# Cross attention and routed FFN on one core: an order of steps of its own for each engine in the attention stage, with routing arithmetic on GpSimd and the value product transposed by VectorE

## Chip, cores and metric

The kernel runs on one core of a Trainium2 chip. The metric is the device time of one execution in microseconds (us). A name such as L292 is line 292 of the kernel before; lines of the changed kernel are marked so. In the profile's rows PE is TensorE, PEld its weight loads, DVE is VectorE, ACT is ScalarE, POOL is GpSimd and SP is SyncE, which here only issues DMAs (SPq in the rows).

## What is computed

128 sequences of 128 tokens with 256 features pass through cross attention (16 heads of 16) and then a mixture of experts: 2 shared experts and, for each token, the best 4 of 16 routed ones. Cut to what matters:

```python
x = x + xattn(layernorm(x), ctx, ctx, Wq, Wk, Wv, Wo)     # softmax(q k^T / 4) v, heads joined, times Wo
h = layernorm(x)
shared = einsum(gelu(h @ shared_up), shared_down)          # 2 experts for every token
probs = softmax(h @ router_w.T); topk_p, topk_i = top_k(probs, 4)
routed = sum over the 4 of gate * (gelu(h @ routed_up[e].T) @ routed_down[e].T)
out = x + shared + routed
```

## The kernel before

The work has two stages on the same core.

**Attention stage.** The 128 sequences (batches n) go in 32 groups g of four (`GT = 4`). One list, `attention_steps()` (L46), is written out by hand, and every engine walks that same list and picks the steps that it has a part in (`run`, L278). Each engine executes its instructions strictly in its own program order and meets the others at semaphores: `fill[b]` and `drain[b]` say that PSUM bank b was written by TensorE and read out by its consumer, and `wait_free` (L275) holds TensorE at a bank until the step before on that bank is drained. The steps: `LN1`/`NA1` normalize x (statistics by VectorE, L750, square root by GpSimd, scaling by ScalarE), `XT` transposes it, `K0 K1 Q0 Q1 VA VB` project, `S` computes scores for the row maxima, `MT` transposes the maxima, `ST` computes the transposed scores less the maxima into banks 4 to 7, ScalarE exponentiates them (L645), `PV` multiplies by the values into bank 5. Then `OTR` (L499, four transposes on TensorE through bank 7 after a ScalarE copy), a division on VectorE (L786), `OT` (L506, two more transposes and a ScalarE copy) and `OP`, the output projection into bank 0, which VectorE adds to x (L798). `LN2`/`NA2` normalize the result into x2 (four buffers), `XT2`, `RL`, `R1`, `RK`, `R2` route: logits, the best four, a running count per expert, and each token's place in the table xs. R2 (L842) is a chain of some 20 small VectorE operations. `SC` (L995) are 512 indirect DMAs from GpSimd that scatter x2's rows into xs; each is also held back until TensorE has come to a certain step (L1005 to L1008).

SyncE issues the plain DMAs, all in one queue. In `LN2(g)` (L311) it waits for y (x plus attention) of group g and stores it, waits for the four `NA2` operations of the group and stores x2, and then issues `make_empty` (L324), a write of 2 MB of zeros for a later part of xs. `LN1(g)` (L299) loads x of group g into one of four buffers; since LN1(g+2) stands in the list where group g is worked on, its load comes behind the stores and the zeros of group g-1 in SyncE's program.

**FFN stage.** Blocks of 512 rows are read from xs, transposed, and multiplied by the expert's weights; 6 shared groups go ahead of the first routed block, then GpSimd gathers four rows for each token and VectorE sums them. VectorE drains the shared groups' down projections here (L928).

The lines that do the waiting of which this document speaks:

```python
def LN1(g):                                   # SyncE, L299
    wait(sp, y_kept[g % 4], 16 * (g // 4)); load_x(g)
def LN2(g):                                   # SyncE, L311
    sp.wait_ge(y_ready, GT * (g + 1));   sp.dma_start(yd ...)
    sp.wait_ge(xn2_ready, GT * (g + 1)); sp.dma_start(x2d ...); make_empty(g + 5)
def LN1(g):                                   # VectorE, L750
    dve.wait_ge(x_in[g % 2], 16 * (g // 2 + 1)); 4 x bn_stats; 4 x bn_aggr
```

Of the kernel before, what the change touches and what calls it, by code (L numbers as in the profile page):

```python
# [8 lines left out]
ALU = mybir.AluOpType  # L9
# [3 lines left out]
P = 128  # L13
# [27 lines left out]
ATT_BANKS = {"S": [0, 1, 2, 3], "K0": [4], "K1": [6], "Q0": [4], "Q1": [6], "VA": [4], "VB": [6], "PV": [5], "OTR": [7],  # L41
             "MT": [5], "OT": [7], "XT": [1, 2], "XT2": [1, 2], "RL": [1], "RK": [1], "OP": [0], "ST": [4, 5, 6, 7]}
# [3 lines left out]
def attention_steps():  # L46

    out = [("LN1", 0), ("NA1", 0), ("XT", 0), ("K0", 0), ("K1", 0), ("Q0", 0), ("Q1", 0), ("VA", 0), ("VB", 0), ("VA", 1), ("VB", 1),
           ("LN1", 1), ("NA1", 1), ("XT", 1), ("S", 0), ("MT", 0), ("ST", 0)]
    for n in range(B):  # L50
        g, i = divmod(n, GT)
        first, second, third, after = {
            0: (("K0", g + 1), ("K1", g + 1), ("RK", g - 2), [("R2", g - 2)]),
            1: (("Q0", g + 1), ("Q1", g + 1), ("XT2", g - 1), [("LN1", g + 2)]),
            2: (("VA", 2 * g + 2), ("VB", 2 * g + 2), ("RL", g - 1), []),
            3: (("VA", 2 * g + 3), ("VB", 2 * g + 3), ("XT", g + 2), [("LN2", g), ("R1", g - 1), ("WS", g)])}[i]
        s = TOPK * (n - 2 * GT - 1)
        out += [("S", n + 1), ("SC", s), first, ("PV", n), ("SC", s + 1)]
        if i == 2:
            out.append(("NA1", g + 2))  # L60
        out += [second, ("OTR", n)]
        if i == 0:
            out.append(("NA2", g - 1))
        out += [("SC", s + 2), third, ("OT", n), ("SC", s + 3), ("MT", n + 1), ("OP", n), ("ST", n + 1)]
        out += after
    g = G
    out += [("RK", g - 2), ("R2", g - 2), ("NA2", g - 1), ("XT2", g - 1), ("RL", g - 1), ("R1", g - 1), ("RK", g - 1), ("R2", g - 1)]
    out += [("SC", k) for k in range(TOPK * (B - 2 * GT - 1), TOPK * B)]
    last = {"SC": TOPK * B, "S": B, "MT": B, "ST": B, "VA": 2 * G, "VB": 2 * G}
    return [(name, n) for name, n in out if 0 <= n < last.get(name, B if name in ("PV", "OTR", "OT", "OP") else G)]  # L70
# [49 lines left out]
ATT = attention_steps()  # L120
# [946 lines left out]
```

## Time and profile before

| what | value |
|---|---|
| median of 3 runs | 2343.75 us (2338.73 to 2350.87) |
| the profiled execution | 2339.02 us, span 2336.8 us |
| busy share of the span: PE, DVE, ACT, POOL | 88%, 67%, 56%, 48% |
| chain that ended last | PE 58%, DVE 12%, POOL 9%, ACT 8%, DMA 7% |
| DMA | 486.46 MB, mean 208 GB/s |

The span is the time from the first instruction to the last in the profile. "Busy" is the union of an engine's instruction times; matmuls are pipelined, so that a row of merged matmuls overlaps the next one, and the spacing of the rows' starts tells what a step takes. The chain is followed back from the last instruction to what released each. A stretch of the page's 40 slices shows DMA share 0.2 to 0.5 up to slice 24, and about 0.9 behind it: the first is the attention stage, the second the FFN stage.

### The profile page before, as it was taken

To read this page: it belongs to the slowest core of one execution; us is meant where nothing else is said; L and a number is where in the kernel's file an instruction comes from. 1 tells how busy PE (TensorE), PEld (TensorE's weight loads), DVE (VectorE), ACT (ScalarE), POOL (GpSimd) and SP (SyncE) were. 2 spreads that over 40 slices of the span, in tenths; PEclk is the share of its full clock that TensorE was granted. 3 is DMA by queue.
4 is the path that set the end of the run, shared out by engine and by line. 5 is a ranking of instruction groups with operands and counts; after the bars stand their busy time and mean duration, and the time that the engine had idled before them with its cause. 6 is when DMAs were issued, how large, how long until landed. Compare 5 with 4: busy or idle time off the path is not lost.

```text
span 2336.8 us, 54349 instructions
## 1 busy us (share of the span) xinstructions
PE 2051.3 (88%) x20646; PEld 1549.3 (66%) x20646; DVE 1574.7 (67%) x4516; ACT 1304.9 (56%) x2364; POOL 1114.2 (48%) x1300
## 2 busy tenths in 40 slices
PE   5888898898888898998998886998999999989982
PEld 3565665665666666666666664687878778877872
DVE  3566666666666666666666656267878788877885
ACT  2445445455444545455545543398777767767772
POOL 1024344444344444444444444306666666666676
PEclk8999999999999999999999997999999999999996
DMA  7234534534534534534444434579999999989995
GB/s 270 78 111 149 167 127 149 176 128 144 178 128 139 174 123 143 174 123 149 164 139 159 143 114 154 202 278 326 332 340 330 338 323 343 332 296 344 328 331 176
DMA packets 242065, 486.46 MB, mean 208 GB/s; under 512 B 25873, under 2 KB 125202, under 8 KB 241810
## 3 DMA queue, kind: packets, MB, share of 16 engines
q1 hardware_dynamic: 192658, 348.71, 43.4%
q0 software_dynamic: 49152, 134.28, 17.3%
q8 instruction: 169, 2.77, 0.5%
q14 instruction: 86, 0.70, 0.1%
HBM read 214.98 MB, written 267.91 MB: 207 GB/s over the span
## 4 chain that ended last, share of the span: by engine, by line
PE 58%; DVE 12%; POOL 9%; ACT 8%; DMA 7%; issue 6%; DVEq 0%; POOLq 0%; SPq 0%; ACTq 0%
POOL gb L1023 9%; PE A L478 7%; PE A L400 7%; PE A L517 7%; PE A L604 6%; PE A L427 6%; DMA gb<-yl,idx 5%; PE A L581 5%; PE A L458 4%; PE A L495 4%; PE A L562 3%; DVE ms L776 3%; PE A L536 2%; ACT ot L657 2%; DVE rr L945 2%
## 5 line engine op out<-in xcount | busy, mean ns | idle before, releaser
L1009 POOL DMA_INDIRECT xs<-xn,idx x512 | 500.9, 978 | 608.2 <-DVE idx L881 187.2
L1023 POOL DMA_INDIRECT gb<-yl,idx x512 | 496.2, 969 | 343.9 <-issue 174.5
L648 ACT ACTIVATE pr<-A 128x512 f32<-128x512 f32 x512 | 264.3, 603 | 386.6 <-PE A L482 386.6
L776 DVE TENSOR_REDUCE ms<-A 128x4 f32<-128x512 f32 x512 | 316.7, 680 | 68.6 <-PE A L458 67.5
L945 DVE SCALAR_TENSOR_TENSOR rr<-gb,gate,rr 128x256 f32<-128x256 f32 x512 | 248.6, 486 | 140.0 <-DMA gb<-yl,idx 121.3
L604 PE MATMUL A<-wt,hh 128*128 128x256 f32 x1144 | 240.7, 294 | 3.7 <-DVE hl L925 3.7
L478 PE MATMUL A<-qt,km 32*128 32x128 f32 x4096 | 220.3, 334 | 0.6 <-DVE mt L796 0.6
L517 PE MATMUL A<-wos,ot 128*128 128x256 f32 x512 | 153.5, 425 | 76.4 <-ACT ot L657 76.4
L478 PEld LDWEIGHTS A<-qt,km 32*128 32x128 f32 x4096 | 183.8, 210 | 49.4 <-issue 45.5
L562 PEld LDWEIGHTS A<-ident,xr 128*128 128x128 f32 x1400 | 161.1, 142 | 82.7 <-issue 68.1
L562 PE MATMUL A<-ident,xr 128*128 128x128 f32 x1400 | 185.1, 276 | 34.0 <-DVE xl L914 29.9
L581 PE MATMUL A<-xh,wt 128*128 128x512 f32 x572 | 207.4, 403 | 0.0
L604 PEld LDWEIGHTS A<-wt,hh 128*128 128x128 f32 x1144 | 187.9, 191 | 4.4 <-DVE hl L925 4.3
L914 DVE TENSOR_TENSOR xl<-A,xh 128x512 fp32r<-128x512 f32 x286 | 182.8, 680 | 11.5 <-ACT xh L699 11.5
L801 DVE TENSOR_TENSOR xb<-A,xb 128x256 f32<-128x256 f32 x128 | 54.3, 424 | 193.0 <-PE A L517 193.0
L719 ACT ACTIVATE yo<-A 128x512 f32<-128x512 f32 x286 | 170.6, 598 | 20.6 <-PE A L604 6.0
L699 ACT ACTIVATE xh<-A 128x512 fp32r<-128x512 f32 x286 | 154.4, 594 | 24.4 <-PE A L562 24.2
L517 PEld LDWEIGHTS A<-wos,ot 128*128 128x128 f32 x512 | 90.8, 197 | 114.9 <-ACT ot L657 107.3
L604 PE MATMUL A<-wt,hl 128*128 128x256 f32 x572 | 161.9, 283 | 0.0
L691 ACT ACTIVATE wt<-wall 128x1024 fp32r x143 | 151.6, 1060 | 18.3 <-issue 14.4
L458 PE MATMUL A<-km,qt 32*128 32x256 f32 x2048 | 151.9, 413 | 1.1 <-ACT xt L638 1.1
L495 PEld LDWEIGHTS A<-pr,vp 128*32 128x32 f32 x4096 | 103.7, 110 | 71.9 <-issue 60.0
(137 smaller groups left out, 3914.1 us busy)
## 6 DMA issues: line engine op xcount, KB each, us to landing
xs<-empty SPq DMA_DIRECT2D x36, 2048.0 KB, 9.9
xr<-xs SPq DMA_DIRECT2D x143, 512.0 KB, 6.0
yl<-yo SPq DMA_DIRECT2D x143, 512.0 KB, 5.7
xb<-in_x SPq DMA_DIRECT2D x32, 512.0 KB, 11.3
cg<-in_ctx_t SPq DMA_DIRECT2D x32, 512.0 KB, 3.9
yd<-xb SPq DMA_DIRECT2D x32, 512.0 KB, 3.3
x2d<-xn SPq DMA_DIRECT2D x32, 512.0 KB, 3.1
xr<-x2d SPq DMA_DIRECT2D x32, 512.0 KB, 6.1
```

The costliest lines, as they stand in the source:

```text
L458: ins = mm(banks[b][:, c * 2 * P:(c + 1) * 2 * P], qt[g % 2][rows, c, i * P:(i + 1) * P], km[g % 2][rows, c, i, :, :].rearrange("p e n -> ...
L478: mm(banks[4 + b][:, r * P:(r + 1) * P], km[g % 2][rows, c, i, e, :], qt[g % 2][rows, c, i * P:(i + 1) * P], start=True, stop=False)
L495: ins = mm(banks[5][32 * q:32 * q + 32, b * P:(b + 1) * P], vp[g % 2][:, i, h, :], pr[:, h, :], start=True, stop=True)
L517: ins = mm(banks[0][:, 0:E], ot[:, c, :], wos[:, c, :], start=c == 0, stop=c == KC - 1)
L562: ins = tr(banks[c][:, q * P:(q + 1) * P], xr[u % 3][:, q, c * P:(c + 1) * P], ident[:, :])
L581: ins = mm(banks[b][:, :], wgt, m, start=k == 0, stop=k == len(passes) - 1)
L604: ins = mm(dst, h, w, start=k == 0, stop=k == len(passes) - 1)
L648: ac(pr[:, 4 * b:4 * b + 4, :].rearrange("p h s -> p (h s)"), banks[4 + b][:, :], ACT.Exp, scale=SCALE)\
L776: v.reduce_max(ms[n % 2][:, b, 0:4], banks[b][:, :].rearrange("p (h t) -> p h t", h=4), AX.X)\
L945: v.scalar_tensor_tensor(y, gb[n % NGB][:, k, :], gate[:, n, k:k + 1], y, ALU.mult, ALU.add)\
L1009: q.indirect_dma_start(xs, bass.IndirectOffsetOnAxis(ap=idx[:, n, k:k + 1], axis=0), x2[g % 4][:, i, :], None).then_inc(sent[g % 4], 16)
L1023: q.indirect_dma_start(gb[n % NGB][:, k, :], None, yl[0:(last_page(g) + 1) * RT, :], bass.IndirectOffsetOnAxis(ap=idx[:, n, k:k + 1], axis ...
```

## The change

Each compute engine gets a cyclic table of steps with an offset for the group or the batch (`("S", 2)` is the batch 4g+2, `("LN1", 3)` the group g+3), and `attention_steps(order)` unrolls it over the groups from g = -8 to G+7, leaving out what does not exist:

```diff
-def attention_steps():
-    ... one list for all engines
+PE_ORDER = [("K1", 1), ("PV", 0), ("MT", 1), ("K0", 1), ("XT", 1), ("OP", 0), ("ST", 1), ("S", 2), ("Q0", 1), ("PV", 1),
+            ("Q1", 1), ("MT", 2), ("XT2", -1), ("OP", 1), ("RK", -2), ("ST", 2), ("S", 3), ("VA", 2), ("VB", 2), ("PV", 2),
+            ("MT", 3), ("RL", -1), ("ST", 3), ("S", 4), ("VB", 3), ("OP", 2), ("PV", 3), ("VA", 3), ("MT", 4), ("S", 5),
+            ("ST", 4), ("OP", 3)]
+ACT_ORDER = [..., ("XT", 1), ("E0", 1), ("E3", 1), ("E1", 1), ("E2", 1), ("NA2", -1), ("Q0", 1), ...]
+DVE_ORDER = [("MS", 1), ("BN", -2), ("BN", -1), ("LN2", -1), ("TA", 0), ("TB", 0), ("RA", -2), ("RB", -2), ("OP", 0),
+             ("RC", -2), ("M0", 2), ("M3", 2), ("M2", 2), ("M1", 2), ("MS", 2), ("TA", 1), ("TB", 1), ("LN1", 3), ("OP", 1),
+             ("RK", -2), ("BN", 0), ...]
+POOL_ORDER = [("SC", -47), ..., ("SC", -43), ("RP", -2), ("SC", -42), ("RG", -2), ("SC", -41), ("WS", 2), ("SC", -40),
+              ("SC", -39), ("LN1", 3), ("SC", -38), ..., ("SC", -33), ("LN2", 0), ("SC", -32)]
+SP_ORDER = [("LN2", -2), ("LN1", 2), ("WS", 1), ("VB", 0)]
```

SyncE: x of groups 0 to 3 is loaded at the start, with a semaphore for each of the four buffers, and from group 4 on in LN1.

```diff
@@ SyncE
             def LN1(g):
-                if g < 2:
+                if g < 4:
                     return
-                wait(sp, y_kept[g % 4], 16 * (g // 4))
+                sp.wait_ge(y_kept[g % 4], 16 * (g // 4))
                 load_x(g)
@@
             load_x(1)
             load_ctx(1)
+            load_x(2)
+            load_x(3)
```

TensorE: OTR and OT go; PV writes bank 5 in a column order that suits 32x32 block transposes; MT moves from bank 5 to bank 7.

```diff
-            def OTR(n): ... 4 transposes
-            def OT(n): ... 2 transposes
             def OP(n):
-                wait_drained(pe, 7, "OT", n)
+                pe.wait_ge(ot_ready, n + 1)
```

VectorE: two block transposes a batch come in; the copies of the values and of MT and the first half of the expert weights' split (WS) go to ScalarE, the second half of WS to GpSimd; R1 and R2 are cut into RA, RB, RC, RK, RM, RS, and what is left out of R2 goes to GpSimd.

```diff
+            def TA(n):
+                wait_filled(dve, 5, "PV", n)
+                wait(dve, o_ready, n)
+                v.transpose(osb[:, :], banks[5][:, :]).then_inc(drain[5], 1)
+            def TB(n):
+                ... reciprocal and multiply, from osb into o
+                v.transpose(ot[:, :, :]..., o[:, :, :]...).then_inc(ot_ready, 1)
             def LN1(g):
-                dve.wait_ge(x_in[g % 2], 16 * (g // 2 + 1))
+                dve.wait_ge(x_in[g % 4], 16 * (g // 4 + 1))
+            def RM(g):
+                dve.wait_ge(r_place, g + 1)
+                ... 4 x v.max(pk, key) ... then_inc(r_key, 1)
```

ScalarE loses the copies of osb and of ot (L653, L657). GpSimd gets RP (15 small operations on 16 or 64 elements a partition, waiting for RK) and RG (the row numbers and three operations on 256 elements, waiting for RM), and SC loses its waits for TensorE:

```diff
@@ GpSimd
-                at = n + 2 * GT + 1
-                if at < B - 1:
-                    ... wait_filled(pool, b, stage, m)
+            def RP(g):
+                pool.wait_ge(r2, 3 * (g + 1))
+                q.tensor_tensor(over[:, :, :], key[:, :, :], bound..., ALU.subtract).then_inc(r_moved, 1)
+                ... 13 more
+                q.tensor_tensor(key[:, :, :], key[:, :, :], gm[g % 2][:, 0:GT, :], ALU.mult).then_inc(r_place, 1)
+            def RG(g):
+                pool.wait_ge(r_key, g + 1)
+                q.tensor_scalar(idx..., pk[:, :, 0:TOPK], -1.0, None, ALU.add).then_inc(r_idx, 1)
+                ... subtract, is_equal, mult on same[128 x 256]
```

How the rows move, at three places.

SyncE's program where group 1 follows group 0, before. xb is the buffer of x, yd and x2d the stored y and x2, empty the zeros, stage the expert weights:

```order
L315 DMA x2d<-xn_3 128x4x256 [waits xn2_ready]
L327 DMA xs<-empty 1024x1x512
L331 DMA stage<-in_wall 128x512 [waits stage_done]
L292 DMA xb<-in_x 128x4x256 [waits y_kept2]
L296 DMA cg<-in_ctx_t 128x2x512 [waits fill6]
L313 DMA yd<-xb 128x4x256 [waits y_ready]
```

And in the change; the line numbers are the changed kernel's:

```order
L328 DMA yd<-xb 128x4x256 [waits y_ready]
L330 DMA x2d<-xn_3 128x4x256 [waits xn2_ready]
L342 DMA xs<-empty 1024x1x512
L305 DMA xb<-in_x 128x4x256 [waits y_kept3]
L346 DMA stage<-in_wall 128x512 [waits stage_done]
L309 DMA cg<-in_ctx_t 128x2x512 [waits fill4,fill6]
```

The load of x still stands behind the store of x2 and the zeros. Before, behind x2 of group g-1 comes x of group g+2; in the change, x of group g+3 (buffer xb3 is loaded behind x2's buffer 3).

VectorE in the second pass of the table, where x of group 4 is first read (x_in0 for the second time); st and mv are LN1's statistics, the xb row is OP(5), and the ms rows are the maxima of batch 6:

```order
L847 STREAM_TRANSPOSE osb<-A 128x512 [waits o_ready,fill5]
L852 RECIPROCAL rd<-osb 128x16 [waits drain5]
L855 TENSOR_TENSOR o<-osb,rd 128x256 [waits ot_ready,rd_ready]
L860 STREAM_TRANSPOSE ot<-o 128x256 [waits fill0,o_ready]
L808 BN_STATS st<-xb 128x6 [waits ln1_mv,x_in0]
L808 BN_STATS st<-xb 128x6 x3
L813 BN_AGGR mv<-st 128x2 [waits ln1_rs,ln1_st]
L813 BN_AGGR mv<-st 128x2 x3
L865 TENSOR_TENSOR xb<-A,xb 128x256 [waits fill0]
L871 BN_STATS st<-xb 128x6 [waits ln2_mv,drain0]
```

LN1 of the group three ahead stands between the transposes of batch 4g+1 and the drain of that batch's OP.

TensorE at the same place of a later pass, OP(4g+1), RK and S(4g+3), without ST and the rows that repeat:

```order
L527 MATMUL A<-wos,ot 128x256 [waits drain0,ot_ready]
L527 MATMUL A<-wos,ot 128x256
L554 MATMUL A<-gm,lowb 128x80 [waits drain1,r_mask]
L556 MATMUL A<-gm,oneb 128x64
L479 MATMUL A<-km,qt 128x256 [waits drain2,drain3,drain1,drain0]
L479 MATMUL A<-km,qt 128x256 x7
```

The scores of batch 4g+3 need banks 0 and 1, which VectorE drains in OP(4g+1) and in RK.

## Rows read from the trace of the kernel before

**Rows 1.** Busy time by stretch: us, PE, PEld, DVE, ACT, POOL, then PEclk, DMA share, GB/s
```profile
955.00:1391.00 436.00, 390.05 (x5058) 278.61 (x5057) 284.10 (x1031) 218.34 (x433) 191.32 (x240) 0.98 0.44 145
1442.00:1490.00 48.00, 38.94 (x155) 27.53 (x156) 17.30 (x80) 15.89 (x28) 35.55 (x38) 0.77 0.62 209
```

**Rows 2.** Line 801, the drain of OP: ns min/median/max, first and last start in us
```profile
L801 DVE TENSOR_TENSOR xb<-A,xb x128: 423/424/426, 56.3 to 1438.9; 128x256 f32<-128x256 f32 x128
```

**Rows 3.** SyncE's timeline in one group: start us, us, line, out<-in
```profile
1021.98 0.53 SPq L327 DMA_DIRECT2D xs<-empty  x1
1022.55 1.17 SPq L292 DMA_DIRECT2D xb<-in_x  x1
```

**Rows 4.** Time to landing: line 292 over the span, and the load near 142 us
```profile
DMA to landing us min/median/max: 4.1/11.3/11.7
...
xb<-in_x SPq DMA_DIRECT2D x1, 512.0 KB, 9.4
```

**Rows 5.** VectorE's timeline in the same group: RK's second half, LN1
```profile
1024.07 0.17 DVE L854 TENSOR_TENSOR base<-A,base 128x16 f32<-128x16 f32 x1
...
1035.22 1.39 DVE L753 BATCH_NORM_STATS2 st<-xb 128x6 f32<-128x256 f32 x4
1036.65 0.38 DVE L758 BATCH_NORM_AGGREGATE mv<-st 128x2 f32<-128x6 f32 x4
```

**Rows 6.** TensorE's timeline in the same group: OP, ST, S, Q0, PV, XT2, V, RL
```profile
1021.87 1.13 PE L517 MATMUL A<-wos,ot 128*128 128x256 f32 x4 [0.66 <-ACT ot L657]
1022.92 0.50 PE L478 MATMUL A<-qt,km 32*128 32x128 f32 x8
...
1024.35 1.15 PE L458 MATMUL A<-km,qt 32*128 32x256 f32 x16
1025.42 1.98 PE L400 MATMUL A<-xt,wqs 128*128 128x512 f32 x4
1027.34 1.08 PE L495 MATMUL A<-pr,vp 128*32 128x128 f32 x32
...
1030.61 1.04 PE L526 MATMUL A<-ident,xn 128*128 128x128 f32 x8
...
1036.72 1.13 PE L427 MATMUL A<-wvs,cg 128*128 128x256 f32 x4
1037.78 1.08 PE L495 MATMUL A<-pr,vp 128*32 128x128 f32 x32
1038.79 1.13 PE L427 MATMUL A<-wvs,cg 128*128 128x256 f32 x4
1039.76 0.60 PE L503 MATMUL A<-ident,osb 128*128 128x128 f32 x4
1040.20 1.86 PE L536 MATMUL A<-wr,t 128*128 128x16 f32 x16
1041.90 0.42 PE L510 MATMUL A<-ident,o 128*128 128x128 f32 x2
```

**Rows 7.** ScalarE's timeline in the same group: NA2, then the exponentials
```profile
1019.48 2.07 ACT L678 ACTIVATE xn<-xb,nb,rs 128x256 f32<-128x256 f32 x4
...
1024.50 2.06 ACT L648 ACTIVATE pr<-A 128x512 f32<-128x512 f32 x4 [2.69 <-PE A L482]
```

**Rows 8.** GpSimd's timeline behind the attention stage: first and last of 36 scatters
```profile
1442.79 1.09 POOL L1009 DMA_INDIRECT xs<-xn,idx  x1 [0.50 <-issue]
...
1488.28 0.96 POOL L1009 DMA_INDIRECT xs<-xn,idx  x1 [0.30 <-issue]
```

**Rows 9.** Groups of instructions by line: count, busy us, mean ns, idle before
```profile
L776 DVE TENSOR_REDUCE ms<-A 128x4 f32<-128x512 f32 x512 | 316.7, 680 | 68.6 <-PE A L458 67.5
...
L466 PE MATMUL A<-ident,ms 128*128 128x128 f32 x128 | 35.7, 279 | 3.1 <-DVE ms L784 3.1
...
L983 POOL TENSOR_TENSOR nb<-ng,rs 128x4 f32<-128x4 f32 x32 | 6.4, 199 | 2.5
...
L969 POOL TENSOR_SCALAR_AFFINE_SELECT sel<-sel 128x512 f32<-128x512 f32 x8 | 5.1, 633 | 1.0
```

More of the change, by code:

```diff
@@ L38 @@
 LAG = 2
-ATT_BANKS = {"S": [0, 1, 2, 3], "K0": [4], "K1": [6], "Q0": [4], "Q1": [6], "VA": [4], "VB": [6], "PV": [5], "OTR": [7],
-             "MT": [5], "OT": [7], "XT": [1, 2], "XT2": [1, 2], "RL": [1], "RK": [1], "OP": [0], "ST": [4, 5, 6, 7]}
+ATT_BANKS = {"S": [0, 1, 2, 3], "K0": [4], "K1": [6], "Q0": [4], "Q1": [6], "VA": [4], "VB": [6], "PV": [5],
+             "MT": [7], "XT": [1, 2], "XT2": [1, 2], "RL": [1], "RK": [1], "OP": [0], "ST": [4, 5, 6, 7]}
 FFN_BANKS = {"TR": lambda u: [0, 1], "U": lambda r: [2 + r % 2], "DN": lambda u: [4 + 2 * (u % 2), 5 + 2 * (u % 2)]}
-def attention_steps():
[L48 to L70, printed above, removed]
@@ L73, in last_page, with attention_steps @@
+PER_GROUP.update({name: GT for name in ("S", "MT", "ST", "PV", "OP", "E0", "E1", "E2", "E3", "M0", "M1", "M2", "M3", "MS", "TA", "TB", "BN")})
+def attention_steps(order):
+    out = []
+    for g in range(-8, G + 8):
+        for name, c in order:
+            each = PER_GROUP.get(name, 1)
+            if 0 <= each * g + c < each * G:
+                out.append((name, each * g + c))
+    return out
 def last_page(g):
@@ L345, in _ @@
                 make_empty(k)
-            run(ATT, {"LN1": LN1, "VB": VB, "LN2": LN2, "WS": WS})
+            run(SP_STEPS, {"LN1": LN1, "VB": VB, "LN2": LN2, "WS": WS})
             def load_unit(u):
@@ L632, in Q1, with values, VA, VB @@
                 wait_filled(act_e, 6, "Q1", g)
+                if g > 1:
+                    wait_filled(act_e, 7, "ST", GT * (g - 1) - 1)
                 ac(qt[g % 2][:, 1, :], banks[6][:, :], ACT.Copy).then_inc(drain[6], 1)
+            def values(n, half, b, stg):
+                g, k = divmod(n, 2)
+                wait_filled(act_e, b, stg, n)
+                if g > 1:
+                    wait_filled(act_e, 5, "PV", GT * (g - 2) + 2 * k + half)
+                ac(vp[g % 2][:, 2 * k + half, :, 0:HD], banks[b][:, 0:E].rearrange("p (h d) -> p h d", h=NH), ACT.Copy)\
+                    .then_inc(drain[b], 1)
+            def VA(n):
+                values(n, 0, 4, "VA")
+            def VB(n):
+                values(n, 1, 6, "VB")
+            def MT(n):
+                wait_filled(act_e, 7, "MT", n)
+                if n > 1:
+                    wait_filled(act_e, 7, "ST", n - 2)
+                ac(mt[n % 2][:, :], banks[7][:, 0:P], ACT.Copy).then_inc(drain[7], 1)
             def XT(g):
@@ L735, in _ @@
             v.memset(one16[:, :], 1.0)
-            for a in (base, bound, shift, taken):
+            for a in (base, bound, taken):
                 v.memset(a[:, :], 0.0)
+            v.memset(shift[:, :], 1.0)
             v.memset(mask[:, 0:1], 0.0)
@@ L1012, in _, with WS @@
+            def WS(g):
+                if g < NRT:
+                    pool.wait_ge(stage_hi, g + 1)
+                    q.tensor_tensor(wall[:, g:g + 1, :, 1, :], stage[g % 2][:, :, :, :], wall[:, g:g + 1, :, 0, :].bitcast(F32), ALU.subtract)\
+                        .then_inc(stage_done, 1)
             pool.wait_ge(const_dve, 3)
-            run(ATT, {"LN1": LN1, "LN2": LN2, "SC": SC})
+            run(attention_steps(POOL_ORDER), {"LN1": LN1, "LN2": LN2, "RP": RP, "RG": RG, "SC": SC, "WS": WS})
@@ L1015, in _ @@
+            pool.wait_ge(r_idx, G)
             for n in range(B):
```

294 lines of the change are left out of this document (172 added, 122 removed), and 6 rows, old and new, of tables (ACT_ORDER, DVE_ORDER).

## Prediction

> **What bounds the kernel now.** I read the busy times by stretch first. In the attention stage TensorE is busy 390.05 of 436 us at a granted clock of 0.98, the others far less (VectorE 284.10, ScalarE 218.34, GpSimd 191.32) [rows 1]: TensorE bounds it, with 46 us of holes in ten groups. Line 801 runs once a batch; its first and last start, 56.3 and 1438.9, give (1438.9 - 56.3) / 127 = 10.89 us a batch, **43.55 us a group** [rows 2]. Of the 2336.8 us the change can touch these 1382.6 and what follows until the first routed block; the FFN stage's instructions are the same. TensorE's timeline shows what a step costs, from start to start; the timelines of SyncE, VectorE and ScalarE in the same group show how x comes in [rows 3, 5, 6, 7].
>
> **TensorE's own work in a pass of the new table.** OP 1021.87 to 1022.92 is 1.05 us, ST then 1.43, S 1.07, Q0 (K0, K1 and Q1 have its form) 1.92, PV 1.01, a value projection 1.06 or 0.97, RL 1.70, XT or XT2 1.04 [rows 6], MT 0.28 [rows 9]. Four batches take 4 x (1.05 + 1.43 + 1.07 + 1.01 + 0.28) = 19.4, K and Q 7.7, the values 4.1, XT and XT2 2.1, RL 1.7. RK has no row of its own here; it lies between 0 and five MTs (1.4), and I take 0.3, since its matmuls are small. **Sum 35.2 us.** What the change removes are OTR (0.44 [rows 6]) and OT (at most 0.42 [rows 6]), 3.4 us a group at most, and the waits behind them. With small waits of 1.3 a pass would be 36.5 us, if nothing else held it.
>
> **What goes to the other engines.** VectorE gets a transpose of 512 and one of 256 elements a batch. The trace has no transpose on it. The nearest row is the reduction of 512 elements from PSUM, 0.680 us [rows 9]; so I take 0.68 and 0.42 (OP's drain of 256 elements, [rows 2]), 4.4 us a group. The low end is half of it, the high end twice. VectorE had 28.4 a group [rows 1]; even with nothing taken off it has 32.8, in the high case 37.2, and it loses four value copies, four MT copies and most of R2. ScalarE, 21.8 a group [rows 1], gives two copies a batch and takes two. Both are costed at nothing, because the pass below is longer than either; without that cover the high case would cost 2 us a group.
>
> GpSimd had 19.1 us a group [rows 1], 16 scatters in it. Back to back they come every (1488.28 - 1442.79) / 35 = 1.30 us for 0.96 busy [rows 8], which adds 5.4. New are RP (15 small operations) and RG (four, three of them on 256 elements). A two-input operation on 4 elements takes 0.199, a one-input one on 512 takes 0.633 [rows 9]: 0.85 ns an element. For two inputs I take twice that, and 0.08 between operations: 0.31 for 64 elements, 0.63 for 256. RP is then 5.0 and RG 2.2 us; the low end is 19 x 0.199 = 3.8 together, the high end twice my value, 14.4. With half an expert-weight subtraction (about 0.5) GpSimd needs 32.2 us a group, under TensorE's 35.2. The waits for TensorE in front of the scatters go; nothing waits for a scatter here, so that is worth nothing.
>
> **The wait that I think decides.** LN1(g+3) stands in VectorE's order behind the transposes of batch 4g+1 and ahead of OP(4g+1). It waits for x of group g+3. SyncE issues that load only behind y(g-1), x2(g-1) and the zeros: the same queue order as before, one group further ahead. x2(g-1) waits for NA2(g-1), which ScalarE does in the same pass g, behind the exponentials of batch 4g+1. Before, the same sequence was: NA2 starts at 1019.48 and ends at 1021.55 [rows 7], the zeros are issued at 1021.98, x at 1022.55 [rows 3], its landing takes 11.3 us in the median [rows 4], so it is there at 1033.9, and LN1 starts at 1035.22 [rows 5]. It just fitted, because two batches lay between. Now VectorE is at LN1 about 1.5 us behind NA2. It must stand until the load lands, and behind it in its order are OP(4g+1) and RK, which drain banks 0 and 1. TensorE needs both for S(4g+3) and stands as well.
>
> So the pass is a loop, and its length the sum around it:
> - from the start of S(4g+3) to the end of ST(4g+5), TensorE: 3 S 3.2, 3 ST 4.3, 3 PV 3.0, 3 MT 0.8, 3 OP 3.2, 4 values 4.1, RL 1.7, K0 and K1 3.8, XT 1.0: **25.1**
> - exponentials 2.06 and NA2 2.07 [rows 7]: **4.1**
> - NA2's end to the issue of x: **1.0** [rows 3, 7]
> - landing: 11.3 in the median with scatters among it, 9.4 in an early group without them [rows 4]. GpSimd will have stopped at RP (it waits for RK) in the second half of the load, so I take **10.8**; ends 4.1 (the shortest of all) and 11.7
> - LN1 1.81 (1035.22 to 1036.65, and 0.38) [rows 5], OP's drain 0.42 [rows 2], RK's two sums 0.4 (the second is 0.17 [rows 5]): **2.6**
>
> **The sum.** The wait exists for the loads of x in groups 4 to 31, 28 passes: 28 x 46.6 = 1305. The other 3.75 of 31.75 passes take 36.5 each: 137. Together 1442 for 1382.6: **+60**. Then the end: before, the last scatter starts 49.4 us behind the last drain of OP [rows 2, 8]. In the table 48 scatters and the RP and RG of two groups lie behind the last LN2: 48 x 1.30 + 2 x 7.2 + 4 = 81 us, 31 later. The six shared groups cover some of it, but VectorE, which drains them, stands at RM behind RP. I take **+20**, ends 0 and 31. From the profiled 2339.0 that gives 2419, say **2420 us**. The profiled execution is 4.7 under the median of the runs, which is within the spread shown.
>
> **Rivals.**
> - *A, x is there in time, faster.* The mechanism is the same LN1 on VectorE, and the point is the landing: if the load landed in the shortest 4.1 us [rows 4], the pass would be 43.6 - 6.7 = 36.9, with small waits 37.5, hardly a hole and no loss of clock: 28 x 37.5 + 137 = 1187, and 2339 - 196 + 20 = 2163. If it did not bind at all, 31.75 x 36.5 = 1159: 2135. For it: the 2 MB of zeros need not delay a load that was issued half a microsecond later, if the DMA engines took them side by side. Against: with the same neighbours the median is 11.3. 14%.
> - *B, GpSimd becomes the bound, slower still.* From RK through RP, RG, ten scatters, LN1 and LN2 to NA2 it takes 5.0 + 2.2 + 13.0 for the scatters + 3.6 for LN1 and LN2 (19.1 less 16 x 0.96) + about 1.3 = 25.1 us, and NA2 wants it 27.2 behind the start of S(4g+3). It decides from RP and RG over 9.3 us. At the high end (14.4) it is 32.3, 5.1 too long, of which the 2.5 of clock already cover half: 28 x 2.6 = 73 and 14 at the end: 2507. 10%. The Trainium skill (GPSIMD Engine Reference, Performance versus the Vector engine) speaks against such a move: two-input arithmetic takes about 2.6 cycles an element there, about twice as long as on VectorE. By its figure, as an estimate, RG would take 0.3 us more, which stays inside the slack.
> - *C, the wait is there but cheap, no change.* Landing 9.4, clock loss 1: a pass of 43.7, 28 x 43.7 + 137 = 1361, less 22, plus 20: 2337. 8%.
>
> **The numbers.** Forecast 68%, A 14%, B 10%, C 8%. About 0.5% (12 us) is what a measurement of this kernel can tell from no change. Slower: forecast and B, 0.78. Same: C, 0.08. Faster: A, 0.14. The forecast's own ends: landing 9.4 to 11.7, clock 1 to 4, end 0 to 31 give about 2345 to 2490 where they don't all fall on one side; B lies at 2507, and half of it is taken in at 2500. A is left out (14%), and a little at the two ends. Range 2340 to 2500.
>
> **What would show it.** The spacing of OP's drains would be 46 to 47 us in four, with one hole of 8 to 10 us in each pass in front of the scores of batch 4g+3, ended by VectorE's RK; VectorE would stand 9 to 10 us in front of LN1's first bn_stats, released by the DMA of x, and its landing would be 10 to 11.5 us. The granted clock would be lower than now in the attention stage. GpSimd would stand at RP. It is wrong if LN1 shows no idle time in front of it, if TensorE is busy over 95% there, or if GpSimd has no idle time at all (then it is B).

## The result and the profile after

| | before | after |
|---|---|---|
| median of the runs, us | 2341.74 (4 runs) | 2399.64 (4 runs, 2398.31 to 2400.74) |
| ratio to before, 95% interval | | **1.024 [1.021, 1.027]** |
| span of the profiled execution, us | 2336.8 | 2397.3 |
| mean granted clock | 0.959 | 0.90 |

The change made the kernel 2.4% slower. First the page of the changed kernel, its busy times and granted clock, and the chain that ended last:

```profile
PE 1946.0 (81%) x19878; PEld 1487.3 (62%) x19878; DVE 1520.5 (63%) x4004; ACT 1262.3 (53%) x2380; POOL 1329.4 (55%) x1924
...
PEclk8999889898888888889889896899999999999996
...
PE 47%; DMA 19%; issue 12%; DVE 9%; POOL 8%; SPq 3%; ACT 3%; DVEq 0%; ACTq 0%; POOLq 0%
DMA xb<-in_x 13%; PE A L614 7%; PE A L448 7%; POOL gb L1123 6%; PE A L591 6%; PE A L479 5%; DMA gb<-yl,idx 4%; PE A L499 4%; PE A L519 4%; PE A L572 4%; PE A L417 3%; PE A L527 3%; DVE rr L1002 2%; PE A L546 2%; SPq L342 2%
```

One entry names the trouble: the load of x (`xb<-in_x`) is 13% of the chain, some 310 us. The busy times by stretch, in the attention stage and behind it (columns: stretch, its length, busy of PE, PEld, DVE, ACT, POOL with instructions, granted clock, DMA share, GB/s), answer to [rows 1]:

```profile
955.00:1391.00 436.00, 344.72 (x4641) 249.71 (x4643) 261.45 (x856) 198.12 (x422) 246.22 (x424) 0.88 0.42 142
1464.00:1554.00 90.00, 52.15 (x204) 36.16 (x205) 16.78 (x65) 19.82 (x34) 60.02 (x90) 0.72 0.52 176
```

TensorE has 91 us of holes for 46, and 0.88 of its clock for 0.98. Next come the drain of OP, as in [rows 2], and by line what the engines waited for (an indented row gives the wait in us and how often):

```profile
L865 DVE TENSOR_TENSOR xb<-A,xb x128: 390/417/425, 60.0 to 1461.7; 128x256 f32<-128x256 f32 x128
...
  DMA xb<-in_x: 309.0, 30
...
  PE A L479: 283.6, 28
...
DMA to landing us min/median/max: 4.0/11.5/12.4
...
L1069 POOL TENSOR_TENSOR over<-key,bound x32: 313/314/337, 156.0 to 1500.4; 128x64 f32<-128x64 f32 x32
...
  DVE taken L932: 338.5, 30
```

VectorE stood 309.0 us, 30 times, in front of LN1's first bn_stats (L808) for x; 28 times TensorE's scores (L479) stood behind it, 10.1 us each; GpSimd stood 338.5 us in front of RP. The 11.5 us is the landing of all 32 loads of x, 11.3 before [rows 4]; for the 28 that follow the first four it is 11.8 (9.1 to 12.4). One pass, engine by engine (VectorE, TensorE, SyncE, ScalarE, GpSimd):

```profile
1009.65 0.45 DVE L860 STREAM_TRANSPOSE ot<-o 128x256 f32<-128x256 f32 x1
1021.12 1.41 DVE L808 BATCH_NORM_STATS2 st<-xb 128x6 f32<-128x256 f32 x4 [11.03 <-DMA xb<-in_x]
...
1022.86 0.39 DVE L865 TENSOR_TENSOR xb<-A,xb 128x256 f32<-128x256 f32 x1
...
1023.42 0.17 DVE L928 TENSOR_TENSOR base<-A,base 128x16 f32<-128x16 f32 x1
...
1023.70 2.09 PE L479 MATMUL A<-km,qt 32*128 32x256 f32 x16 [10.10 <-DVE xb L865]
1025.71 3.78 PE L448 MATMUL A<-wvs,cg 128*128 128x256 f32 x8
...
1034.13 1.10 PE L479 MATMUL A<-km,qt 32*128 32x256 f32 x16
...
1008.70 0.53 SPq L342 DMA_DIRECT2D xs<-empty  x1
1009.27 1.17 SPq L305 DMA_DIRECT2D xb<-in_x  x1
...
1006.19 2.08 ACT L729 ACTIVATE xn<-xb,nb,rs 128x256 f32<-128x256 f32 x4
...
1024.18 0.31 POOL L1069 TENSOR_TENSOR over<-key,bound 128x64 f32<-128x64 f32 x1 [12.37 <-DVE taken L932]
...
1027.36 0.30 POOL L1089 TENSOR_TENSOR key<-key,gm 128x64 f32<-128x64 f32 x1
```

NA2 ends at 1008.27, the zeros go out at 1008.70, x at 1009.27; VectorE comes to LN1 at 1010.09, and x is there at 1021.12. Behind the hole the scores take 2.09 us where they take 1.10 some ten us later: TensorE is at 1.2 GHz. This pass is 46.5 us long, from one load of x to the next, and the 27 of them last 42.6 to 46.7, each with a granted clock of 0.85 to 0.89.

**Where the 60.5 us of the span went.** The first OP drain is 3.7 us later (60.0 for 56.3). From first to last it is 1401.7 us for 1382.6: **+19.1**. From the last drain to the first routed matmul it is 1557.99 - 1461.7 = 96.3 us, for 68.1: **+28.2**. What remains of the FFN stage is 839.3 for 829.8, +9.5, though its instructions are the same; in the kernels below, which share it too, it lies between 829 and 841. Both values lie in that spread, and no run here shows another cause.

### The profile page after: what moved, and what is told of

It is laid out like the page before. It is cut to its first block, busy times and chain, and to the rows that moved or that the text cites. A ratio compares the mean times of both kernels' runs of the same rounds, so it can differ in the third digit from the quotient of the medians.

```text
span 2397.3 us, 55514 instructions
## 1 busy us (share of the span) xinstructions
PE 1946.0 (81%) x19878; PEld 1487.3 (62%) x19878; DVE 1520.5 (63%) x4004; ACT 1262.3 (53%) x2380; POOL 1329.4 (55%) x1924
## 4 chain that ended last, share of the span: by engine, by line
PE 47%; DMA 19%; issue 12%; DVE 9%; POOL 8%; SPq 3%; ACT 3%; DVEq 0%; ACTq 0%; POOLq 0%
DMA xb<-in_x 13%; PE A L614 7%; PE A L448 7%; POOL gb L1123 6%; PE A L591 6%; PE A L479 5%; DMA gb<-yl,idx 4%; PE A L499 4%; PE A L519 4%; PE A L572 4%; PE A L417 3%; PE A L527 3%; DVE rr L1002 2%; PE A L546 2%; SPq L342 2%
## 5 line engine op out<-in xcount | busy, mean ns | idle before, releaser
L1061 POOL DMA_INDIRECT xs<-xn,idx x512 | 506.6, 989 | 168.0 <-issue 152.1
L479 PE MATMUL A<-km,qt 32*128 32x256 f32 x2048 | 170.7, 454 | 283.6 <-DVE xb L865 283.6
L479 PEld LDWEIGHTS A<-km,qt 32*128 32x128 f32 x2048 | 109.8, 216 | 303.5 <-DVE xb L865 289.2
L656 ACT ACTIVATE vp<-A 128x256 f32<-128x256 f32 x128 | 46.6, 390 | 448.9 <-PE A L448 448.9
L808 DVE BATCH_NORM_STATS2 st<-xb 128x6 f32<-128x256 f32 x128 | 44.9, 414 | 309.0 <-DMA xb<-in_x 309.0
L1069 POOL TENSOR_TENSOR over<-key,bound 128x64 f32<-128x64 f32 x32 | 10.1, 315 | 338.5 <-DVE taken L932 338.5
L499 PE MATMUL A<-qt,km 32*128 32x128 f32 x4096 | 191.2, 302 | 1.0 <-ACT mt L669 0.5
L448 PE MATMUL A<-wvs,cg 128*128 128x256 f32 x512 | 171.6, 480 | 11.4 <-ACT vp L656 11.4
L499 PEld LDWEIGHTS A<-qt,km 32*128 32x128 f32 x4096 | 167.9, 187 | 15.6 <-issue 11.7
## 6 DMA issues: line engine op xcount, KB each, us to landing
xb<-in_x SPq DMA_DIRECT2D x32, 512.0 KB, 11.5
```

The costliest lines, as they stand in the source:

```text
L448: ins = mm(banks[b][:, 0:E], cg[g % 2][:, c, i * P:(i + 1) * P], wvs[:, c, :], start=c == 0, stop=c == KC - 1)
L479: ins = mm(banks[b][:, c * 2 * P:(c + 1) * 2 * P], qt[g % 2][rows, c, i * P:(i + 1) * P], km[g % 2][rows, c, i, :, :].rearrange("p e n -> ...
L499: mm(banks[4 + b][:, r * P:(r + 1) * P], km[g % 2][rows, c, i, e, :], qt[g % 2][rows, c, i * P:(i + 1) * P], start=True, stop=False)
L1061: q.indirect_dma_start(xs, bass.IndirectOffsetOnAxis(ap=idx[:, n, k:k + 1], axis=0), x2[g % 4][:, i, :], None).then_inc(sent[g % 4], 16)
```

## The experiments

Spans below go by the same marks: the loop is the first to last drain of OP, the tail the last drain to the first routed matmul.

**The x load ahead of the x2 store and the zeros** (in LN2 on SyncE):

```diff
                 sp.wait_ge(xn2_ready, GT * (g + 1))
+                if g + 4 < G:
+                    sp.wait_ge(y_kept[g % 4], 16 * (g // 4 + 1))
+                    load_x(g + 4)
                 sp.dma_start(token_rows(x2d, g)
...
     def LN1(g):
-        if g < 4:
-            return
-        sp.wait_ge(y_kept[g % 4], 16 * (g // 4))
-        load_x(g)
+        return
```

> The changed kernel with one edit on SyncE: the load of x for the group four ahead is issued right behind the wait for NA2, ahead of the store of x2 and of the 2 MB of zeros. Theory (the pass is a loop through the landing of x, 11.5 us in the changed kernel because it lies behind the zeros): the landing falls to 4 to 5 us and the issue comes 1.0 us earlier, so the loop is 7.5 to 8 us shorter; the pass goes from 45.5 to 37.5 to 38.5 us, VectorE's idle time in front of LN1 from 309 us to 60 to 110, and the whole to 2170 to 2210 us. Rival (GpSimd's RP and RG, or the order of the banks, hold the pass, and VectorE only happens to stand at LN1): the wait moves on to RM or to a bank, and the time stays within 1% of 2400.

Measured 2138.34 us, ratio 0.9117 [0.9085, 0.915]. The drain, VectorE's wait at L808, and one load with the LN1 that waits for it:

```profile
L865 DVE TENSOR_TENSOR xb<-A,xb x128: 390/416/426, 60.1 to 1209.2; 128x256 f32<-128x256 f32 x128
...
  DMA xb<-in_x: 80.6, 30
...
965.11 0.37 SPq L305 DMA_DIRECT2D xb<-in_x  x1
...
969.59 1.41 DVE L808 BATCH_NORM_STATS2 st<-xb 128x6 f32<-128x256 f32 x4 [2.67 <-DMA xb<-in_x]
```

This trace does not record when x lands, but VectorE waits for each of the 28 loads, so LN1's start bounds it: 4.2 to 5.8 us behind the issue, 4.5 in the median, where it was 11.9. The same 512 KB ahead of the 2 MB of zeros land that much sooner, and 261 us are gone. The theory's direction holds; the result is 32 us below the range given. The landing is not why: with an issue 1.0 us earlier it makes 8.3 us a pass, and the pass went from 45.5 to 36.3, 9.2. The sum had left out the clock. The 27 passes had a grant of 0.85 to 0.89; now 10 have 1.00 (35.2 us long in the mean) and 17 have 0.95 or 0.96 (36.9).

**LN1 later in the pass.** The load stays where it is; the waiting instruction moves, on VectorE and on GpSimd:

```diff
-  ("TB", 1), ("LN1", 3), ("OP", 1),
+  ("TB", 1), ("OP", 1),
...
-  ("M3", 4), ("MS", 4), ("OP", 2),
+  ("M3", 4), ("MS", 4), ("LN1", 3), ("OP", 2),
...
-  ("SC", -39), ("LN1", 3), ("SC", -38)
+  ("SC", -39), ("SC", -38)
...
-  ("SC", -33), ("LN2", 0), ("SC", -32)
+  ("SC", -33), ("LN1", 3), ("LN2", 0), ("SC", -32)
```

> The changed kernel with SyncE as it is; LN1 of the group three ahead goes further back in the pass, on VectorE from behind TB(4g+1) to behind the maxima of batch 4g+4, on GpSimd to just ahead of LN2. The landing stays 11 to 11.5 us. Theory (only the place of the wait in VectorE's order matters, since OP, RK and with them the banks of the scores are queued behind it): no engine stands for x any more, TensorE is the bound at 35 to 37 us a pass, the granted clock in the attention stage is back at 0.98 or more, and the whole is 2120 to 2170 us. Rival 1 (the landing itself or DMA traffic bounds the pass): it stays above 43 us and the whole above 2350. Rival 2 (GpSimd is next, 32 us by the estimate): GpSimd shows no idle time, the pass is 38 to 41 us and the whole 2200 to 2290.

Measured **2113.7 us, ratio 0.9022 [0.8994, 0.905]**; x still took 11.1 us to land in the median and up to 11.9, and hardly anybody waited for it (the last row is the x loads' own):

```profile
L865 DVE TENSOR_TENSOR xb<-A,xb x128: 390/424/425, 60.0 to 1174.0; 128x256 f32<-128x256 f32 x128
...
  DMA xb<-in_x: 0.9, 1
...
DMA to landing us min/median/max: 4.0/11.1/11.9
```

The loop is 1114.0 us, 35.1 a group; the time is 6 us under the range given. With the landing unchanged and 286 us gone, what cost was not the transfer's length but what was queued behind its wait.

**Both orders together.**

> The x load ahead of the x2 store and the zeros, and LN1 of group 4g+3 later in the pass, together. After the first alone VectorE still stood 80.6 us for x before LN1, after the second alone 1.1 us. If all that the x load cost was this wait, the two together give what the second gives, 2108 to 2118, TensorE's own work being the limit of 35.1 us a group. Rival: the landing of 11 us disturbed something else too (the x2 store, the scatters' queue), and the two together are 5 to 15 us faster, or slower because the x2 rows and zeros are now stored later.

Measured 2103.22 us, ratio 0.8974 [0.8957, 0.8991]. That is 10 us better than the later LN1 alone, as the rival had it. This trace has x's own landing, for the 28 loads behind the first four:

```profile
DMA to landing us min/median/max: 4.0/4.5/6.2
```

The profiled executions differ by 16.6 us: 9.1 in the loop (1104.9 for 1114.0), 6.2 in the rest of the FFN stage, which both share, and 1.2 in the tail. In the loop the passes at a grant of 1.00 are alike, 34.6 us long here (21 of 27) and 34.5 with the later LN1 alone (19 of 27). The difference lies in the others: 6 of 35.8 us here, 8 of 36.7 there. The three kernels at the end, under the tail, divide in the same way, 6 slower passes with the early load and 8 with the late one. So the late load goes with more and longer stretches at the low clock; by what path stays open.

**Idle matmuls in the hole.** To price the clock apart from the hole, matmuls of 512 columns on idle data go ahead of S(4g+3):

```diff
+            def FILL(g):
+                if 0 < g < G - 3:
+                    wait_free(pe, 5, "PV", GT * g + 2)
+                    for _ in range(18):
+                        mm(banks[5][:, :], ident[:, :], wqs[:, :, :].rearrange("p c e -> p (c e)"), start=True, stop=True)
...
-  ("ST", 2), ("S", 3),
+  ("ST", 2), ("FILL", 0), ("S", 3),
```

> The changed kernel with 18 matmuls of 512 columns more, whose results nobody reads, on TensorE in each of 28 passes, in the hole in front of the scores of batch 4g+3 (about 8 of its 10 us). The wait for x stays. Theory of the clock (behind the hole TensorE works at 1.2 GHz for some us, and that lies on the loop): the clock stays full behind the hole, the pass is 1.5 to 2.5 us shorter, the whole 2330 to 2360 us, with more work done. Rival (what runs slowly behind the hole is covered by other engines' work, so the clock costs nothing): within 0.5% of the changed kernel, 2388 to 2412. If the extra matmuls run over the end of the hole it would be slower than that.

> Nine matmuls of 512 columns on idle data, about 7.9 us by the 0.87 us that one took with eighteen of them, stand on TensorE behind the scores' transposes and ahead of the scores of group 4g+3, in the hole of 10.1 us, from which the first 1.2 us are spent on their own wait. TensorE is then busy in the hole and does nothing useful. If the low granted clock behind the hole is what the hole costs beside its own length, the pass of 45.5 us becomes 1.5 to 2.5 us shorter, and the time 2330 to 2360. Rival: what the matmuls behind the hole lose to the clock is made good by slack elsewhere in the loop (it runs through the x load and VectorE), and the time stays at 2388 to 2412.

Both kernels held eighteen, so the second tested nothing new: it was meant to hold nine and its count had not been changed. They measured 2556.03 us (ratio 1.0917 [1.0881, 1.0953]) and 2555.19 (1.0915 [1.0886, 1.0945]): the eighteen take 15.7 us and run over the hole's end, so neither tells anything about the clock, only that the same kernel repeats within 1 us. The third has nine:

> The two runs before this one with idle matmuls in the hole both had eighteen of them, which took 15.7 us and ran over the end of the hole of 10.1 us. This one has nine, about 7.9 us, from 1.2 us behind the hole's start, so that they end inside it. If the half clock behind the hole lengthens the pass, it falls from 45.5 by 1.5 to 2.5 us, and the time to 2330 to 2360. Rival: what the clock costs TensorE is slack elsewhere in the loop, and the time stays at 2388 to 2412.

Measured **2365.56 us, ratio 1.0089 [1.0059, 1.0118]**. TensorE's timeline from the idle matmuls on (one such matmul leaves two records, so nine are x18):

```profile
1032.99 7.99 PE L494 MATMUL A<-wqs,ident 128*128 128x512 f32 x18 [1.15 <-ACT pr L696]
1042.02 1.15 PE L479 MATMUL A<-km,qt 32*128 32x256 f32 x16 [1.04 <-DVE xb L871]
1043.09 1.99 PE L448 MATMUL A<-wvs,cg 128*128 128x256 f32 x8
...
1049.93 2.06 PE L479 MATMUL A<-km,qt 32*128 32x256 f32 x16
```

Adding useless work to TensorE made the kernel 34 us faster: the low clock did cost, 34 / 28 = 1.2 us a pass in the mean, though less than the 1.5 to 2.5 expected. The time lies between the two ranges. S and the two values behind the hole take 1.15 and 1.99 instead of 2.09 and 3.78, 2.7 us less, and the clock from 955 to 1391 is 0.98. But in this pass scores 8 us later run at 2.06 us, and so it is in half of the passes. Three in a row, from one load of x to the next (columns as in [rows 1]):

```profile
540.54:584.52 43.98, 41.21 (x492) 27.47 (x491) 26.88 (x89) 20.70 (x44) 26.54 (x44) 1.00 0.46 151
584.52:630.17 45.65, 42.86 (x492) 28.96 (x491) 26.79 (x89) 20.80 (x44) 27.78 (x46) 0.96 0.43 142
630.17:673.77 43.60, 41.24 (x492) 27.50 (x491) 26.87 (x89) 20.18 (x43) 25.43 (x43) 1.00 0.43 143
```

Of the 27, 13 have a grant of 1.00 and last 43.6 us in the mean, 14 have 0.96 and last 45.1; unfilled, all have 0.85 to 0.89 and last 45.5. A pass that keeps its full clock is thus 1.9 us shorter, which is inside what was expected; the filling reached it in half of them.

**The VectorE transposes alone**, in the order of before (OTR, OT and ScalarE's two copies out, the two transposes where VectorE had OTR, PV's column order as in the change; MT stays in bank 5, behind PV):

> The kernel before with one part of the change: the value product goes through VectorE's two block transposes instead of TensorE's six transposes and ScalarE's two copies; the common order of steps, the routing on VectorE and the rest are as before (two of the waits in front of the scatters name PV and MT instead of the transposes that are gone). Theory (TensorE is the bound before, and waits for the round trips of OTR and OT): TensorE is relieved of 0.7 to 0.9 us a batch and of part of the 1.1 us of waits, so 43.55 us a group goes to 38.5 to 41 us and the whole to 2180 to 2270 us; x still lands in time only if the pass is not shorter than the landing, so some of it can come back as a wait at LN1 (there were 1.3 us to spare). Rival (the transposes on VectorE cost as much as they save, since TensorE waits for them one after the other): within 1% of the kernel before.

Measured 2378.64 us, ratio 1.0165 [1.013, 1.0199]: slower than both expectations. TensorE's waits from 955 to 1391 (us in total, times, longest), of OP for the transposed product and of MT for bank 5:

```profile
PE A L506 <- DVE ot L781: 28.3, 39, 0.8
PE A L466 <- DVE osb L770: 26.9, 22, 2.4
```

and the same stretch by its busy times, as in [rows 1]:

```profile
955.00:1391.00 436.00, 379.13 (x4589) 263.51 (x4593) 315.08 (x1087) 178.18 (x342) 184.41 (x232) 0.89 0.43 142
```

TensorE did less and was held no less: 55 us of waits in ten groups, before 46, now all for VectorE, which is 72% busy here. The clock fell from 0.98 to 0.89 in this stretch, and from 0.96 to 0.92 over 83 to 1391 us, and the loop is (1463.9 - 53.7) / 127 = 11.10 us a batch for 10.89. How much of that is the waits and how much the clock, no run separates. So the transposes gain nothing by themselves in the old order. Half of the waits are MT's for bank 5 (L466), which VectorE now drains; the changed kernel has MT in bank 7, so that part may be this kernel's own, which no run tests.

**The removed work put back**, on top of both orders: six transposes of 128 by 128 on idle data ahead of each MT.

> On top of both orders (2103.2 us): six transposes of 128 by 128 on idle data stand in front of each MT, the work that OTR and OT were for TensorE, without their waits and copies. TensorE is busy 98% of the pass there. If its own work is the limit, each of the 127 batches is 0.7 to 0.9 us longer, a pass 38 to 38.6 us, and the time 2190 to 2220. Rival: the removed work lay in holes that are there anyway, and the time is under 2140; then the orders alone made the gain and the transposes on VectorE little of it.

Measured 2160.37 us, ratio 0.923 [0.9205, 0.9255]; the six took 0.65 to 0.71 us from start to start, and TensorE's waits shrank:

```profile
1012.89 0.87 PE L488 MATMUL A<-ident 128*128 128x128 f32 x6
1013.60 0.27 PE L489 MATMUL A<-ident,ms 128*128 128x128 f32 x1
```

Of its waits from 400 to 1100:

```profile
PE A L479 <- DVE xb L867: 8.6, 19, 0.8
```

The loop is 1161.2 us for 1104.9, 0.44 a batch: some 0.68 of work, less what earlier waits (20.3 us in the same window without it) absorb; slower passes by the clock are rarer too, 3 of 27 for 6. Between the two expectations: of the 240 us that both orders win, the transposes off TensorE are worth at least 57, in this order, since the waits and ScalarE's copies that went with them were not put back.

**Places and gates on VectorE** again, on top of the later LN1: RP and RG around RM, none on GpSimd.

> On top of the later LN1 (2113.7 us): the places and gates (RP, RG) are done by VectorE around its maxima RM, and GpSimd has none. VectorE has idle time in the attention stage, and a pass of 35.1 us has some 22 us of VectorE's work; the 20 instructions add about 3 us. If GpSimd's part matters only in the tail, the loop stays at 35.1 us a group to within 0.3, and the stretch from the last drain to the first routed matmul gets 10 to 15 us shorter: 2098 to 2108. Rival: the added VectorE work delays its drains for TensorE, the pass grows to 36 to 37 us, and the time is 2125 to 2160.

Measured 2167.64 us, ratio 0.9241 [0.9216, 0.9266]: the rival, and 8 us beyond its range. Groups of VectorE's and TensorE's instructions, 400 to 1200:

```profile
L479 PE MATMUL A<-km,qt 32*128 32x256 f32 x1360 | 112.5, 447 | 36.7 <-DVE ls L886 29.6 <-DVE xb L865 6.4 <-ACT pr L690 0.7
...
L979 DVE TENSOR_TENSOR same<-same,prob 128x256 f32<-128x256 f32 x22 | 9.4, 425 | 0.8
```

RP and RG took VectorE about 3 us a pass (860.38 to 862.2 for RP, 1.8 us, and 1.3 for RG, whose last product is the second row); the logits' subtraction (L886) stood behind them, the scores behind that, and the pass grew from 35.1 to (1248.3 - 60.4) x 4 / 127 = 37.4 us. The tail got 11 us shorter, 85.4 for 97.1. The clock has a part in it: 22 of the 27 passes have a grant of 0.91 or 0.95, where the later LN1 alone has 8; the five at 1.00 last 36.4 us for 34.5. So the move to GpSimd is worth some 54 us, the clock with it, although it is slower there: RP took 3.5 us (1024.18 to 1027.66 in the changed kernel).

**The tail.** In the changed kernel VectorE stands at RM for 18.29 us behind GpSimd, so the routing table is late; and the scatters end late. SyncE's wait for the table:

```profile
SPq L381 <- DVE tab L965: 39.0, 1, 39.0
```

the table's DMA, by its line:

```profile
L381 SPq DMA_DIRECT2D td<-tab x1: 332/332/332, 1511.7 to 1511.7; - x1
```

and from the timeline the last scatter, and TensorE's wait for x2 rows:

```profile
1538.58 0.96 POOL L1061 DMA_INDIRECT xs<-xn,idx  x1 [0.30 <-issue]
...
1520.45 1.97 PE L572 MATMUL A<-ident,xr 128*128 128x128 f32 x8 [22.15 <-DMA xr<-x2d]
```

Behind the last drain the table leaves after 50.0 us (before 22.6) and the last scatter starts after 76.9 (before 49.4 [rows 2, 8]): both 27.5 later, and so is the tail. Fifty scatters stand there for 36, 14 x 1.265 = 17.7 us; the rest is mostly the two RP and RG between them, 7.5 us each time with the wait for RM. Three kernels tell the table and the scatters apart. First RP and RG of the last two groups pulled ahead of scatters, on top of the later LN1:

> On top of the later LN1 (2113.7 us): GpSimd keeps RP and RG, but for the last two groups they are moved ahead of the scatters that stand before them in its order, so that VectorE's wait for the key in front of its last maxima ends sooner and the routing table leaves SP's queue sooner. If this wait is what made the tail longer than before, the first routed matmul comes 8 to 20 us sooner and the time is 2094 to 2106; the loop is untouched. Rival: the scatters that are now later set when the first routed rows can be read, or the group's own chain does, and the time stays at 2109 to 2118.

Measured 2112.82 us, ratio 0.9024 [0.9001, 0.9048]: the rival, no change, though the table left 31.8 us behind the last drain where it had been some 50. Then every scatter nine places earlier in GpSimd's table, on top of both orders:

```diff
-POOL_ORDER = [("SC", -47), ..., ("SC", -43), ("RP", -2), ("SC", -42), ("RG", -2), ("SC", -41), ...
+POOL_ORDER = [("SC", -38), ..., ("SC", -34), ("RP", -2), ("SC", -33), ("RG", -2), ("SC", -32), ...
```

> On top of both orders (2103.2 us): every scatter stands nine places earlier in GpSimd's order, so that the first of group g-2 follows its row numbers at once. Behind the last drain of the output projection there are then 41 scatters for 50, 9 x 1.265 = 11.4 us less until the first routed matmul. If the backlog of scatters sets the end of the attention stage, the time is 2088 to 2096. Rival, as in the run with the last places pulled forward: something else ends at the same time, and it stays at 2099 to 2107; or the scatters hold RP and the pass gets longer, over 2110.

Measured 2100.66 us, ratio 0.8982 [0.8958, 0.9007], the rival again, though the last scatter started 65.7 us behind the last drain (78.9 in the kernel before this one). TensorE's longest waits in the tails of the two, first the one then the other:

```profile
1262.23 1.97 PE L572 MATMUL A<-ident,xr 128*128 128x128 f32 x8 [17.20 <-DMA xr<-xs]
```

```profile
1223.04 1.97 PE L572 MATMUL A<-ident,xr 128*128 128x128 f32 x8 [22.47 <-DMA xr<-x2d]
```

With the table early, TensorE ran out of shared groups and waited for scattered rows; with the scatters early, it waited for x2d, whose loads stand behind the table in SyncE's queue, and then had the shared groups still to do. Both at once:

> Pulling the last places forward alone left the end as it was (TensorE then waited 17.2 us for rows of xs, which the scatters deliver), and so did the earlier scatters alone (TensorE then waited 22.5 us for rows of x2d, whose loads stand behind the routing table in SyncE's queue, and ran the shared groups without a break from there). So each should be the other's cover. Here both are done: on top of the earlier scatters, RP and RG of group 31 stand behind scatters 483 and 484. The table should leave 13 us sooner, the first routed matmul come 10 to 14 us sooner than in either, about 83 us behind the last drain for 96, and the time be 2085 to 2095. Rival: a third thing ends there too, and the time stays at 2098 to 2106.

Measured **2094.67 us, ratio 0.8939 [0.8917, 0.8962]**. The table's DMA and the first routed matmul, by line, then TensorE's wait in the timeline:

```profile
L381 SPq DMA_DIRECT2D td<-tab x1: 332/332/332, 1208.0 to 1208.0; - x1
...
L591 PE MATMUL A<-xh,wt x572: 387/395/628, 1255.6 to 2046.2; 128*128 128x512 f32 x191
```

```profile
1216.24 1.97 PE L572 MATMUL A<-ident,xr 128*128 128x128 f32 x8 [7.74 <-DMA xr<-x2d]
```

The tail is 1255.6 - 1171.6 = 84.0 us, where it was 95.9 with both orders and 96.5 with the earlier scatters alone. The ten other kernels here that have RP and RG on GpSimd have tails of 95.9 to 98.7 us, so 12 us is clear of their spread. The total shows less: the median is 6 us lower than that of the earlier scatters, the intervals of the two ratios overlap a little, and the two profiled executions take the same time, since here the loop happened to take 1111.2 us for 1104.4 and the rest of the FFN stage 4.7 more. The first routed matmul comes 18.1 us behind the last scatter here; it was 18.7 in the kernel before and 19.4 in the changed one, and 30.8 with the earlier scatters alone, where the table held it. Whether the scatters are what the tail waits for again is not tested. This is the fastest version tried: **10.6% under before, where the change as made is 2.4% over it.**

## Why the prediction was right, and where its sizes were off

It said slower, 2420 us in 2340 to 2500; it came out at 2399.6.

- *The mechanism.* The wait at LN1 for x, with OP(4g+1) and RK behind it and S(4g+3) behind those, is there 28 times in the form forecast: 11.03 us on VectorE in the pass shown (forecast 9 to 10), 10.1 on TensorE in the mean (8 to 10). The two kernels that take it away in different ways each win over 260 us, so it is shown, not only argued.
- *The pass.* Forecast 46.6; 27 intervals between x loads give (1327.85 - 99.19) / 27 = 45.5. NA2 2.08 (2.07) and the issue 1.0 (1.0) fit. The landing was under-sized, 11.8 for 10.8: that GpSimd stops scattering did not shorten it. TensorE's part was over-sized by about as much: from S(4g+3) to the end of ST(4g+5) it took 26.7 us in the pass shown (1023.70 to 1050.44), 24.0 without the 2.7 that the low clock costs there, for 25.1. The clock's term held, 2.5 us: the stretch behind the hole loses 2.7, and passes freed of the low clock were 1.9 shorter, though the filling as a whole gave back only 1.2. By the Trainium skill (TensorE: Matmul & The Clock Gate, HAM oscillation) a long hole puts the array back to half rate; the 2.09 for 1.10 us behind the hole agrees, and so does the gain from matmuls that only fill it.
- *The other passes.* Forecast 36.5; (1401.7 - 28 x 45.5) / 3.75 = 34.0, and 34.8 to 35.1 where nothing stands. TensorE's own sum was about 1 us too long: OP takes 0.87 to 0.99 us from start to start here, not 1.05, and MT 0.11 to 0.20, not 0.28, which was its busy time and not its spacing; the small waits were below the 1.3 taken. Together the loop was mis-sized by 40 us, 30 of it from the pass.
- *GpSimd.* RP took 3.5 us for 5.0, RG 2.6 for 2.2: 6.1 for 7.2. Its bound (rival B) was never near; with x in time (the later LN1) it still stood in front of RP, 102.6 us in 30 times for the 338.5 of the changed kernel. That it takes longer there than on VectorE agrees with the Trainium skill (GPSIMD Engine Reference, Performance versus the Vector engine: about twice for two inputs) in direction, and in size for the whole: 3.5 for 1.8 us in RP, 2.6 for 1.3 in RG. Single two-input operations differ less, 0.31 for 0.22 us at 64 elements, 0.61 to 0.73 for 0.42 at 256. The rule spoke against the move and the runs for it: an engine twice as slow that has time to spare is still the better place.
- *Transposes.* VectorE's took 0.71 and 0.45 us in the mean, for 0.68 and 0.42 taken.
- *The end.* Forecast +20, measured +28.2. The step that was wrong here is "the six shared groups cover some of it": they cover nothing, because the table's delay holds their own loads.
- *Rival A* named 2135 to 2163 for x in time. The two kernels that make it so gave 2138 and 2114, so the mechanism's price was right, and the end that "did not bind at all" too cautious by 21 us.
- *The removed matmuls.* The sum counts them as 3.4 us a group at most and the waits behind them as gone. On their own, in the old order, they won nothing; in the new order putting them back costs 1.8 us a group. The forecast did not need this, since the wait for x set the pass.
- That the total is so near, 20 us off, is in part luck: the loop was 40 us too long, the tail 8 too short, and 13 us (first drain, FFN stage) were not in the sum. Inside the pass, too, two errors of 1 us (landing, TensorE's part) cancelled.

## To carry to other kernels

When each engine gets its own order, look at each wait on a DMA and ask what stands behind it on that engine: moving LN1 by 18 places in VectorE's order (and on GpSimd with it) was worth 286 us, with the transfer as slow as ever (11.1 us for 11.5). Put a small load that somebody waits for ahead of a large store that nobody waits for in the same queue. If removing a suspected limit gives nothing, remove the one beside it too before dropping the theory: here the table and the scatters were each the other's cover.

## What the runs showed of the chip that I had not expected

- A 512 KB load issued just behind a 2 MB store on one queue (0.57 us in the pass shown) landed after 11.8 us in the median (9.1 to 12.4); ahead of it, in the kernel of both orders, after 4.5 (4.0 to 6.2).
- Taking matmuls off TensorE while its waits stayed went with a lower granted clock (0.92 for 0.96 over the attention stage) and a longer time, 2378.64 us for 2341.14.
- With hardly a hole, scores still take 2.06 us for 1.10 now and then (1017.21 us in the kernel of both orders), at a mean grant of 0.99 there. Counted by pass the grant is 1.00 or about 0.95, and a pass at 0.95 is 1.2 us longer (35.8 for 34.6). What brings this on stays open.
- One-input operations on GpSimd were not cheaper than two-input ones: is_equal on 256 elements took 0.86 us, the subtraction ahead of it 0.61; VectorE took 0.32 and 0.42 (routing on VectorE).
